# First tiles of the pooling: what stands in front of a branch and what behind it

## The reference

```
x = x + attn(layernorm(x))      # 4 layers: norm, silu, complex scan along the tokens, norm, two-layer MLP;
                                # width 128, 1024 -> 128 ahead of it, layer norm, 128 -> 1024 behind it (Wout, bout)
x = x + xattn(layernorm(x), ctx)
    # mask: of each channel's 256 context values, the k = 154 greatest
    # crucial = mask * y, rest = (1 - mask) * y; maxima and means of both over the tokens,
    # a small convolution, batch norm and sigmoid over them; y times one gate or the other
x = x + ffn(layernorm(x))       # 8 experts, the best 2 for each token
```

## Time and profile before

| | us |
|---|---|
| median of 3 runs | 1164.08 (1160.13 to 1164.36) |
| the profiled execution's own time | 1166.08 |
| its span on the core | 1164.0 |
| TensorE busy | 1056.5 (91%) |
| VectorE busy | 564.1 (48%) |
| ScalarE busy | 402.8 (35%) |
| GpSimd busy | 493.5 (42%) |
| experts' matmuls (line 1985) | 509.9 |

### The profile page before, as it was taken

The page is one execution under the profiler, slowest core; times in us unless marked ns, Lnnn a source line. Parts: engine busy times, 40 slices in busy tenths (PEclk is TensorE's granted clock), DMA queues, the critical chain, the costliest instruction groups (busy, mean ns, idle before and its releaser), DMA issues. The chain is left out here.

```text
span 1164.0 us, 13959 instructions
## 1 busy us (share of the span) xinstructions
PE 1056.5 (91%) x3739; PEld 584.2 (50%) x3740; DVE 564.1 (48%) x1655; ACT 402.8 (35%) x1142; POOL 493.5 (42%) x662
## 2 busy tenths in 40 slices
PE   6787889999999879789992999999999999999995
PEld 6785455555545435336992444444444444444442
DVE  5646578888787868988847211111111121111111
ACT  2435787787776317757720000000000000000000
POOL 3833567667575100006702533444433334444331
PEclk9878899999999889988555999999999999999998
DMA  7310111110000232002686337373735536373332
GB/s 302 134 55 0 47 46 37 44 48 1 1 1 1 73 145 73 1 1 91 260 318 239 87 72 216 72 223 83 230 77 149 139 74 214 75 226 86 81 73 37
DMA packets 38465, 120.29 MB, mean 103 GB/s; under 512 B 6220, under 2 KB 9351, under 8 KB 38408
## 3 DMA queue, kind: packets, MB, share of 16 engines
q1 hardware_dynamic: 25592, 79.77, 18.6%
q0 software_dynamic: 12816, 39.86, 15.7%
HBM read 82.91 MB, written 36.70 MB: 103 GB/s over the span
## 5 line engine op out<-in xcount | busy, mean ns | idle before, releaser
L1985 PE MATMUL bank<-T,X 128*128 x1184 | 509.9, 594 | 2.9 <-DVE X L2029 2.9
L1985 PEld LDWEIGHTS bank<-T,X 128*128 128x128 f32 x1184 | 225.5, 191 | 286.7 <-issue 286.7
L2043 DVE TENSOR_SCALAR X<-bank,col_p 128x512 f32<-128x512 f32 x37 | 27.8, 751 | 401.9 <-PE bank L1985 401.9
L2009 ACT ACTIVATE X<-bank,col_p 128x512 f32<-128x512 f32 x37 | 25.4, 687 | 504.8 <-PE bank L1985 504.8
L1938 POOL DMA_INDIRECT X<-x_nrm,col_s x156 | 150.0, 962 | 75.8 <-issue 46.9
L1947 POOL DMA_INDIRECT out_dram<-X,col_d x37 | 60.0, 1621 | 264.8 <-DVE X L2043 251.1
L449 POOL TENSOR_TENSOR T<-T 128x8 f32<-128x8 f32 x216 | 93.3, 432 | 16.3
L822 ACT ACTIVATE M<-X,T 128x256 bf16<-128x256 f32 x200 | 98.5, 498 | 0.0
L458 POOL TENSOR_TENSOR rs<-ve,neg_half 128x4 f32<-128x4 f32 x36 | 45.7, 1270 | 91.1 <-DVE ve L961 90.9
L634 PE MATMUL bank<-nat,T 128*128 128x512 f32 x128 | 69.4, 672 | 7.9 <-ACT X L810 5.4
L216 POOL TENSOR_TENSOR late<-late,neg_half 128x1 f32<-128x1 f32 x32 | 17.5, 546 | 125.7 <-DVE late L212 125.7
(11 more groups left out here) (330 smaller groups left out, 1529.0 us busy)
## 6 DMA issues: line engine op xcount, KB each, us to landing
T<-in_L_ffn_expert_w_dram SPq DMA_DIRECT2D x8, 4096.0 KB, 17.7
out_dram<-X SPq DMA_DIRECT2D x17, 512.0 KB
M<-in_x_dram SPq DMA_DIRECT2D x16, 512.0 KB, 7.4
X<-in_x_dram SPq DMA_DIRECT2D x16, 512.0 KB, 5.2
x_nrm<-H SPq DMA_DIRECT2D x16, 512.0 KB, 3.6
T<-in_ctx_dram SPq DMA_DIRECT2D x9, 512.0 KB, 3.6
X<-x_nrm,col_s POOLq DMA_INDIRECT x156, 3.7
X<-in_ctx_dram SPq DMA_DIRECT2D x4, 512.0 KB, 7.1
```

The source lines that it names most:

```text
L1985: mm = nc.tensor.matmul(bank[2 * u + n][:, :], xgt[u][:, k, :], Tf[:, ds(odd * D + (k * N + n * BANK), BANK)], start=(k == 0), stop=(k == ...
```

## The change

`EARLY` is 8 where it was 4, and a new number `FIRST_TILES` = 2 takes its old place in the loops. Eight rows of x are loaded in the first block, for which the sync queue also waits for `z_mm`. TensorE and ScalarE do tiles 0 and 1 in the first block, where they did four; tiles 2 and 3 come at the start of the third block, ahead of `turned(0)`. VectorE computes the statistics of tiles 0 and 1, and GpSimd their powers, at the end of the first block, between the check and the cast. The check is one operation that compares each count with 154 and sums over the channels; `off_i` can now be up to 128 x 64. Row t from 10 on waits for the tile eight before it. The workspace of the slow selection starts four rows later.

```diff
-        EARLY = 4
+        EARLY = 8
+        FIRST_TILES = 2
         def load_row(sp, t):
-            if t >= RQ + EARLY:
+            if t >= RQ + FIRST_TILES:
                 sp.wait_ge(x1_done, 2 * (t - RQ) + 2)
...
                 sp.wait_ge(o_mm, VISITS)
+                sp.wait_ge(z_mm, VISITS)
                 for t in range(EARLY):
                     load_row(sp, t)
...
+                for t in range(FIRST_TILES):
+                    ln_pow(pool, 0, t)
...
                 pe.wait_ge(b_split, 12)
-                for t in range(EARLY):
+                for t in range(FIRST_TILES):
                     products(pe, t)
-                pe.wait_ge(off_set, 4)
+                pe.wait_ge(off_set, 1)
...
-                for t in range(EARLY):
+                for t in range(FIRST_TILES):
                     rows(act, t)
...
-                v_.tensor_scalar(off, m_cnt, -float(KC), None, ALU.add).then_inc(off_set, 1)
-                hold(dve, off_set, 1)
-                v_.tensor_tensor(off, off, off, ALU.mult).then_inc(off_set, 1)
-                hold(dve, off_set, 2)
-                v_.tensor_reduce(off_one, off, AX.X, ALU.max).then_inc(off_set, 1)
-                hold(dve, off_set, 3)
-                v_.tensor_scalar(off_any, off_one, 0.25, None, ALU.is_gt).then_inc(off_set, 1)
+                v_.tensor_scalar(off, m_cnt, float(KC), 0.0, ALU.not_equal, ALU.add, accum_out=off_any).then_inc(off_set, 1)
+                for t in range(FIRST_TILES):
+                    hold(dve, x1_done, 2 * t + 2)
+                    ln_stats(dve, 0, t)
                 hold(dve, off_mm, 1)
...
-        free = TPC * D
+        free = EARLY * D
...
-                for t in range(NT):
+                for t in range(FIRST_TILES, NT):
                     ln_pow(pool, 0, t)
...
+                for t in range(FIRST_TILES, LAG + 1):
+                    products(pe, t)
                 for t in range(NT + LAG + 1):
...
+                for t in range(FIRST_TILES, LAG + 1):
+                    rows(act, t)
                 for t in range(NT + LAG + 2):
...
-                    if t < NT:
+                    if FIRST_TILES <= t < NT:
                         hold(dve, x1_done, 2 * t + 2)
                         ln_stats(dve, 0, t)
```

More of the change, by code:

```diff
@@ L292, in decoder_kernel @@
         m_cnt, off = in_sel(B * KD), in_sel(B * KD)
-        off_any, off_one = in_sel(1), in_sel(1)
+        off_any = in_sel(1)
         off_i = sb("off_i", [P, 1], I32)
@@ L1237, in decoder_kernel @@
         w_all = Xf[:, free + CT * D:free + CT * D + KD * WA].rearrange("p (i s) -> p i s", i=KD)
-        assert free + CT * D + KD * WA <= 3 * free
-        top_all = Xf[:, 3 * free:3 * free + KD * 8].rearrange("p (i s) -> p i s", i=KD)
+        assert free + CT * D + KD * WA <= NT * D - KD * 8
+        top_all = Xf[:, NT * D - KD * 8:NT * D].rearrange("p (i s) -> p i s", i=KD)
         all_in, all_tp, all_w, all_max, all_rep, all_mask = (sem(n) for n in ("all_in", "all_tp", "all_w", "all_max", "all_rep", "all_mask"))
@@ L1244, in _ @@
             def _(sp):
-                missed = sp.value_load(off_i[0:1, 0:1], min_val=0, max_val=P)
+                missed = sp.value_load(off_i[0:1, 0:1], min_val=0, max_val=P * B * KD)
                 with sp.If(missed > 0):
@@ L1253, in _ @@
             def _(pe):
-                missed = pe.value_load(off_i[0:1, 0:1], min_val=0, max_val=P)
+                missed = pe.value_load(off_i[0:1, 0:1], min_val=0, max_val=P * B * KD)
                 with pe.If(missed > 0):
@@ L1267, in _ @@
                 v = nc.vector
-                missed = dve.value_load(off_i[0:1, 0:1], min_val=0, max_val=P)
+                missed = dve.value_load(off_i[0:1, 0:1], min_val=0, max_val=P * B * KD)
                 with dve.If(missed > 0):
```

## The result

Twenty runs of each kernel gave 1174.3 us for the changed one (1160.0 to 1179.1) and 1161.7 for the kernel before (1158.7 to 1167.9). The medians are 12.6 us apart, where the forecast was 4.9, and 1174.3 lies 1.0 us above the stated range. The comparison of the runs, which isn't one of medians, gives a ratio of 1.008, with a 95% interval of 1.006 to 1.010: slower by 9.3 us, about twice the forecast. The spread tells as much as the median. The kernel before is scattered over 9 us; of the changed one 18 runs lie from 1173.3 to 1179.1, and two lie at 1160.0 and 1161.3, with nothing between. The profiled execution took 1173.76 us, its span is 1171.7.

A forecast was written before the change was run, and what follows sets the result against it. VectorE bounds the pooling, whose start waits for TensorE's tile 4. Branch 2.1 us later, TensorE's stretch 16.3 us instead of 13.5: +4.9 on 1164.08 gives 1169.0 us, range 1163.9 to 1173.3.

The forecast's parts named there:

- What bounds it: Pooling is held by VectorE, but its start, `crucial(0)`, waits for tile 4's products on TensorE and ScalarE's copy.
- The check and the statistics in front: End of first block: one-operation check, two tiles' statistics (3.6 us) and GpSimd's power bring the branch 2.1 us later.
- Two tiles' products behind the branch: TensorE behind the branch: six half tiles and two turned tiles, 13.5 us at full clock, without a wait.
- The clock in the front: TensorE behind the branch: half clock for 5.4 us, costing 2.8 us (2.1 to 3.8).
- four returns behind the 5.4: Times from TensorE's work to its clock's rise, read from the slices: 5.0, 7.3, 5.7 and 4.0 us; middle 5.4.
- TensorE's resumption: First instruction behind the branch: taken to cost TensorE nothing beyond VectorE's value, with 3.3 us as upper end.
- its rival: TensorE resumes late behind the branch, up to 3.3 us: +5.8 to +8.2, with late clock +9.2; chance 0.12.
- A shift of `crucial(0)` is a shift of the end.: Everything behind the pooling's start follows in program order, so its 4.9 us delay reaches the end.
- my own sign of being wrong: Wrong if the stages behind the pooling change in length; line 1700's start and the branch's delay were further signs.
- The one on the VectorE side: VectorE bounds the start of pooling, so early statistics gain: −1.5 us, perhaps −6; chance 0.04.
- The one on the clock: Clock does not hold TensorE back behind the branch and a later wait absorbs 1.0 us: +1.1; chance 0.11.
- The wait of 1.02 us: The one wait after `crucial(0)`, at 448.11; the clock rival had it absorb part of the shift.

The follow-up runs named there:

- the delayed changed kernel: Changed kernel with two more small unneeded operations ahead of its check: 1159.6 us against 1161.8 for the kernel before, ratio 0.998.
- the wide forms: Router's second part as 256-column matmuls, kernel before and changed: 1160.9 and 1166.9 us; with the last three result copies on VectorE, 1153.3 and 1160.7 us.
- The twice delayed kernel before: Kernel before with line 1222's operation and its wait done three times instead of once: 1162.4 us against 1165.3, ratio 0.998.

## Why the prediction was right or wrong

*What bounds it.* Right for the front: in every kernel `crucial(0)` waited for tile 4's copy, 4.4 to 5.4 us of idle before it, and the pooling behind it kept its length (83.8 to 84.3 us).

*The check and the statistics in front.* Right. The branch came 2.4 us later for a forecast of 2.1, and the end of GpSimd's power does count. Counted from the first product, `crucial(0)` came within 0.4 us of the forecast.

*Two tiles' products behind the branch.* Right: 15.8 us from the branch to tile 4's copy, forecast 13.5 + 2.8 and 0.1 to the copy, 16.4; the 0.6 us less are the clock's.

*The clock in the front.* Mis-sized: the rise came 4.3 us after TensorE's start, not 5.4, so 2.2 us were lost where I had 2.8. One of the four returns behind the 5.4 was misread: at 524.15 the clock was still at 2.4 GHz (0.88 in its slice) and fell some 0.6 us later, so that the 4.0 us there are not all at the low clock. The two deviations, +0.3 and −0.6, have opposite signs: front +4.56, forecast +4.9.

*TensorE's resumption.* Right: 422.36, with VectorE. The rule of the Trainium skill that I weighed there (Runtime: NRT & Kernel Launch, Instruction fetch mechanics) shows no cost for TensorE in this trace beyond what VectorE has, and its rival falls; whether the place behind the branch lay outside the two pages, no run shows. The upper end of my range, 1173.3, rested on that rival; that the measured time came so near to it is luck.

*"A shift of `crucial(0)` is a shift of the end."* This step failed. I had looked for operations that start by an earlier clock and had not read the granted clock of the stage from 540 to 610 us, although the page's strip reads 55 from 553 us on. In that stage TensorE's clock falls under the eight-column matmuls and makes it the bound, and where it comes back changes with a shift of under 1 us. The profiled execution lost 5.3 us there, and my own sign of being wrong, a stage behind the pooling that changes in length, came true. That this loss comes from the clock and not from the change's work is shown by the delayed changed kernel (0.7 us later at the branch, 14.7 us faster); the wide forms, with distances of 6.0 and 7.4 us, bear it out in part. How the 12.6 us between the medians divide is not shown in full: 4.6 are the front, the profiles show 5.3 in the residual stage, and the base of the forecast, the median of three runs, was 2.4 us above that of twenty.

*The rivals.* The one on the VectorE side falls with the 4.42 us of idle. The one on the clock held that the clock costs next to nothing in the front; it cost 2.2 us, and it falls. The wait of 1.02 us that it would have used up fell to 0.64, and the pooling as a whole gave back 0.5. All of them watched the front alone. Slower by over 0.5% had 0.31, and it came; what took it there, the residual stage, was in none of them.

*Open.* Why 18 of 20 runs of the changed kernel meet the bad case, while the kernel before is scattered. Of the kernels with the second part as it was, the two with products 2 and 3 behind the branch and no delay have most runs in one close group and two runs 12 us below it. The twice delayed kernel before is split as well, more widely: four runs from 1156.0 to 1158.5, at a mean granted clock of 0.932 or 0.933, and six from 1162.2 to 1168.5, at 0.923 to 0.926. In the two kernels with the close group TensorE works without a wait from the branch on; that this ties the later falls of the clock to it is argued, not shown, and the delayed changed kernel, which does the same, had no run above 1160.1. The single check alone and the eight early rows alone weren't tried.

## What to carry to other kernels

Work of an engine that idles in front of a barrier is free there. Moved behind it, it can cost most of its length: here two tiles' products, 7.8 us at full clock, made the front 6.7 us longer (42.1 against 35.4), and the statistics that VectorE made in front of the branch were then worth nothing. Before a shift of some microseconds is taken to be passed on to the end, read the granted clock of every later stage in which TensorE is near the bound: where it falls and rises by itself, a small shift can be worth more than the edit, of either sign (here 0.7 us of delay and 14.7 us of time). Hold the clock there first, then compare the edits.

## What the runs showed of the hardware

Busy wasn't enough for the clock: in the changed kernel TensorE was busy 4.00 of 4.00 us in the stretches from 550 us on, with eight-column matmuls behind 128x128 weight loads and transposes, and was granted 0.50. With 256-column matmuls in their place, busy 1.9 to 4.0 of 4.00 us, it kept 1.00 in nearly all stretches. With two 512-column matmuls added for each tile the clock came back at times (0.84 in one stretch, 0.50 in others) and wasn't held.

The fall is worth a factor of 1.73 on the eight-column second part (3.94 to 6.83 us) and about 1.9 on the turning back (1.94 us at 533 us of the kernel before, 3.65 at the low clock).

The changed kernel's runs fall into two groups some 13 us apart, and the one sign in the record that goes with it is the mean granted clock: 0.931 and 0.932 in the two at 1160 and 1161 us, 0.914 to 0.922 in the others.
